# Graph network on one core: the source-order row numbers found in two pieces of columns

## The reference

```python
h = x @ W_in2f
Wij = (ssp(rbf @ Wf1 + bf1) @ Wf2 + bf2) * dist_cut     # rbf: 64 attributes of an edge, dist_cut: its weight
m = segment_sum(h[idx_j] * Wij, idx_i, num_segments=n)  # called with idx_i = src, idx_j = dst
m = ssp(m @ Wo1 + bo1) @ Wo2 + bo2
```

## Time and profile before

| | us |
|---|---|
| median of 3 runs | 6600.42 (6594.85 to 6607.0) |
| the profiled execution | 6596.57 |
| its span | 6594.8 |
| PE / DVE / ACT / POOL busy in the span | 4219.8 / 3130.8 / 1818.7 / 4481.3 |
| POOL's 416 source scatters (L570), busy | 455.7, mean 1.10 |

### The profile page before, as it was taken

How to read it: one execution, slowest core, us unless ns; L and a number is a source line. 1 busy time by engine, 2 the same in 40 slices (tenths; PEclk the granted TensorE clock), 3 DMA queues, 4 the chain that set the end, 5 groups by cost and what they waited for, 6 DMA issues and landing times. The chain is left out here.

```text
span 6594.8 us, 75926 instructions
## 1 busy us (share of the span) xinstructions
PE 4219.8 (64%) x20428; PEld 2957.2 (45%) x20491; DVE 3130.8 (47%) x6389; ACT 1818.7 (28%) x4089; POOL 4481.3 (68%) x4303
## 2 busy tenths in 40 slices
PE   3000788888876666577697555455578867886554
PEld 2000566666544544366595333333344445554333
DVE  9500455555458888866645322232234444442223
ACT  1000566666435555366373000000000000000000
POOL 3777777777668888455421777677677757776775
PEclk6555899999889899799898677766778889987786
DMA  3111222222146666455201555555566644444333
GB/s 86 45 53 53 70 74 75 75 75 74 23 149 211 211 212 213 131 144 148 63 1 64 162 161 163 152 161 163 145 187 199 206 134 148 147 149 103 102 99 94
DMA packets 450732, 812.01 MB, mean 123 GB/s; under 512 B 144428, under 2 KB 300041, under 8 KB 443916
## 3 DMA queue, kind: packets, MB, share of 16 engines
q0 software_dynamic: 209808, 566.12, 30.4%
q1 hardware_dynamic: 240636, 242.29, 11.6%
HBM read 650.48 MB, written 157.63 MB: 123 GB/s over the span
## 5 line engine op out<-in xcount | busy, mean ns | idle before, releaser
L1455 POOL DMA_INDIRECT p_rows<-table,idx_s x1320 | 1285.4, 974 | 574.3 <-issue 377.0
L1500 PE MATMUL p_psA<-p_rows,p_hot 128*128 128x256 bf16 (+1 forms) x4840 | 928.5, 358 | 722.6 <-DMA p_rows<-table,idx_s 534.3
L1500 PEld LDWEIGHTS p_psA<-p_rows,p_hot 128*128 128x128 bf16 (+1 forms) x4840 | 636.1, 137 | 987.9 <-issue 840.2
L570 POOL DMA_INDIRECT rec_s<-p_rec_out,p_row_s x416 | 455.7, 1095 | 223.1 <-issue 126.2
L584 POOL DMA_INDIRECT p_space<-h_table,p_space x440 | 474.2, 1078 | 134.1 <-issue 134.1
L1455 POOL DMA_INDIRECT p_rows<-rel_table,edge_d x440 | 430.7, 979 | 178.9 <-issue 130.1
L1275 POOL DMA_INDIRECT p_rows<-rel_table,edge_d x440 | 437.0, 993 | 161.4 <-issue 133.2
L654 PE MATMUL p_psW<-p_wf,p_upto 128*128 128x256 f32 x1760 | 461.7, 421 | 118.2 <-DVE p_upto L803 117.4
L1739 POOL DMA_INDIRECT p_kg<-kv_table,edge_d x440 | 424.5, 965 | 146.4 <-issue 111.0
L376 POOL DMA_INDIRECT rec_d<-edge_d,norm x416 | 410.9, 988 | 158.3 <-issue 125.9
L1876 DVE TENSOR_REDUCE sums<-p_psM 128x8 f32<-128x1024 f32 x440 | 516.9, 1215 | 2.1 <-PE p_psM L1802 1.8
(11 more groups left out here) (342 smaller groups left out, 8803.2 us busy)
## 6 DMA issues: line engine op xcount, KB each, us to landing
v_sorted<-p_kg SPq DMA_DIRECT2D x110, 512.0 KB, 4.2
p_val<-v_sorted SPq DMA_DIRECT2D x110, 512.0 KB, 3.7
rel_table<-p_o SPq DMA_DIRECT2D x50, 1024.0 KB
p_rows<-table,idx_s POOLq DMA_INDIRECT x1320, 3.1
p_space<-rec_s SPq DMA_DIRECT2D x110, 136.0 KB, 2.1
p_rows<-rel_table,edge_d POOLq DMA_INDIRECT x880, 2.8
p_rec_out<-edge_attr SPq DMA_DIRECT2D x103, 128.0 KB, 2.3
table<-p_o SPq DMA_DIRECT2D x50, 192.0 KB
```

The costliest lines, as they stand in the source:

```text
L570: pool.indirect_dma_start(g.rec_s_rows, bass.IndirectOffsetOnAxis(ap=row_s[:, n * U + u:n * U + u + 1], axis=0), rec_out[q][:, u, :], None ...
L1455: pool.indirect_dma_start(rows[q][:, u, :], None, table, bass.IndirectOffsetOnAxis(ap=idx(n * U + u), axis=0))\
L1500: step = pe.matmul(psA[:, bass.ds(at[u], D)], hot[q][:, u, :], rows[q][:, u, c * D:(c + 1) * D], start=False, stop=(c == terms - 1), skip_ ...
```

## The change

`place_edges` takes a first and a last column (by default all), and works on these alone; the correction of the last column is made only by the piece that has it. The call for the source order becomes two: columns 0 to 31 (FIRST = 8 chunks of 4), then 32 to 415, with a signal of `placed` behind each. The wait for the types and weights (`rest_in`), which stood between the placing and the signal, now stands ahead of the first piece. POOL starts with the first signal, and waits for the second one ahead of the scatters of chunk 8. ACT's wait for the first signal stays as it is. The call for the target order is unchanged.

```diff
+FIRST = 8
-def place_edges(dve, link, g, m, row_out):
+def place_edges(dve, link, g, m, row_out, c0=0, c1=None):
     EC, NB, NT = g.EC, g.NB, g.NT
-    ti = m.tmp_i[:, :]
+    c1 = EC if c1 is None else c1
+    cols = slice(c0, c1)
+    ti, pos, part = m.tmp_i[:, cols], m.pos_f[:, cols], m.part_f[:, cols]
     for b in range(NB):
-        slot = m.part_f if b else m.pos_f
-        of_b = slice(b * EC, (b + 1) * EC)
-        link(dve.scalar_tensor_tensor(out=slot[:, :], in0=m.upto[:, of_b], scalar=m.shift[:, b:b + 1], in1=m.mask[:, of_b],
-                                      op0=ALU.add, op1=ALU.mult))
+        of_b = slice(b * EC + c0, b * EC + c1)
+        link(dve.scalar_tensor_tensor(out=part if b else pos, in0=m.upto[:, of_b], scalar=m.shift[:, b:b + 1],
+                                      in1=m.mask[:, of_b], op0=ALU.add, op1=ALU.mult))
         if b:
-            link(dve.tensor_tensor(m.pos_f[:, :], m.pos_f[:, :], m.part_f[:, :], ALU.add))
+            link(dve.tensor_tensor(pos, pos, part, ALU.add))
...
-    last = row_out[:, EC - 1:EC]
-    link(dve.tensor_tensor(last, last, g.beyond[:, :], ALU.add))
+    if c1 == EC:
+        last = row_out[:, EC - 1:EC]
+        link(dve.tensor_tensor(last, last, g.beyond[:, :], ALU.add))
...
                     pool.wait_ge(brought[q], 16 * (n // few + 1) + 16 * (n == sends - 1))
                     pool.wait_ge(noted, n + 1)
+                    if n == FIRST:
+                        pool.wait_ge(placed, 2)
...
                 find_last(dve, link, g, m, last_tile, ended)
-                place_edges(dve, link, g, m, row_s[:, :])
                 dve.wait_ge(rest_in, 64)
+                place_edges(dve, link, g, m, row_s, 0, FIRST * U)
+                dve.sem_inc(placed, 1)
+                place_edges(dve, link, g, m, row_s, FIRST * U)
                 dve.sem_inc(placed, 1)
```

More of the change, by code:

```diff
@@ L286, in order_blocks @@
     link(dve.tensor_tensor(m.jump[:, 1:NB], m.order[:, 1:NB], m.order[:, 0:NB - 1], ALU.subtract))
-def place_edges(dve, link, g, m, row_out):
+def place_edges(dve, link, g, m, row_out, c0=0, c1=None):
     EC, NB, NT = g.EC, g.NB, g.NT
-    ti = m.tmp_i[:, :]
+    c1 = EC if c1 is None else c1
+    cols = slice(c0, c1)
+    ti, pos, part = m.tmp_i[:, cols], m.pos_f[:, cols], m.part_f[:, cols]
     for b in range(NB):
-        slot = m.part_f if b else m.pos_f
-        of_b = slice(b * EC, (b + 1) * EC)
-        link(dve.scalar_tensor_tensor(out=slot[:, :], in0=m.upto[:, of_b], scalar=m.shift[:, b:b + 1], in1=m.mask[:, of_b],
-                                      op0=ALU.add, op1=ALU.mult))
+        of_b = slice(b * EC + c0, b * EC + c1)
+        link(dve.scalar_tensor_tensor(out=part if b else pos, in0=m.upto[:, of_b], scalar=m.shift[:, b:b + 1],
+                                      in1=m.mask[:, of_b], op0=ALU.add, op1=ALU.mult))
         if b:
-            link(dve.tensor_tensor(m.pos_f[:, :], m.pos_f[:, :], m.part_f[:, :], ALU.add))
-    link(dve.tensor_copy(ti, m.pos_f[:, :]))
+            link(dve.tensor_tensor(pos, pos, part, ALU.add))
+    link(dve.tensor_copy(ti, pos))
     link(dve.tensor_scalar(ti, ti, P - 1, None, ALU.bitwise_and))
-    link(dve.tensor_copy(m.part_f[:, :], ti))
-    link(dve.tensor_copy(ti, m.pos_f[:, :]))
+    link(dve.tensor_copy(part, ti))
+    link(dve.tensor_copy(ti, pos))
     link(dve.tensor_scalar(ti, ti, 7, None, ALU.arith_shift_right))
-    link(dve.scalar_tensor_tensor(out=row_out, in0=m.part_f[:, :], scalar=float(NT), in1=ti, op0=ALU.mult, op1=ALU.add))
-    last = row_out[:, EC - 1:EC]
-    link(dve.tensor_tensor(last, last, g.beyond[:, :], ALU.add))
+    link(dve.scalar_tensor_tensor(out=row_out[:, cols], in0=part, scalar=float(NT), in1=ti, op0=ALU.mult, op1=ALU.add))
+    if c1 == EC:
+        last = row_out[:, EC - 1:EC]
+        link(dve.tensor_tensor(last, last, g.beyond[:, :], ALU.add))
 def find_blocks(dve, link, g, m, plan, found, signal):
```

## The result

Over eight runs of each the changed kernel takes 6623.06 us (6619.68 to 6629.2), the kernel before 6598.17 (6594.39 to 6607.0): 1.0038 times as long, 95% interval 1.0028 to 1.0048. The forecast was 6601.6, from 6590 to 6613, with 0.87 for "within 0.2%". It is slower beyond that. The profiled execution took 6620.07 us, its span 6618.3, which is 23.5 more than before.

The account below looks back on a forecast made before the run. POOL's source scatters were taken as the bound until about 700 us: DVE 10.7 us later, less 9.5 us for 7.4 scatters' lead, gives +1.2 us on the median 6600.42, so 6601.6 us, range 6590 to 6613.

Parts of the forecast that it names:

- The two pieces: DVE's row numbers computed as 32 then 384 columns: 45.5 us against 34.8, so DVE 10.7 us later.
- the upper price: DVE's product on 32 columns at 0.25 us instead of 0.194: DVE 12.2 us later, adding 0.7 us to the sum.
- The first scatter, 16 scatters: POOL starts at 83.9, held by SP's blank records, 16.4 us earlier; 16 scatters at 1.31 us reach 104.9.
- SP: SP's in-order queue still issues chunk 4's load at 122.13, behind fills and stores; it lands 7.3 us later, at 129.4.
- the standstill: POOL stops at 104.9 for chunk 4's attributes and goes on at 130.4: 25.5 us, new.
- The estimate of 2.3 us: Chunk 4's load landing in 2.3 us, not 7.3; the sum would be -1.6 us instead of +1.2.
- The step that failed: POOL's scatters beside DVE's comparisons after the restart: one every 2.27 us, 16.9 from 130.4 to 168.8.
- the slower ones: Cases slower by over 0.2%: SP slowed, chance 0.04, and shifts of DVE's later code, chance 0.02.
- Rival 2: SP's fills slowed by the early scatters, chunk 4's load 21 us later: 6614 us and more; chance 0.04.
- Rival 1: Chunk 4's load comes by 105, so POOL's early start meets no attribute limit: 15.1 us faster, 6585; chance 0.07.
- the sum: Change in the last source scatter's time; with no attribute limit, 10.7 - 25.8 = -15.1 us.

Follow-up runs that it names:

- reordered_third: Changed kernel with SP's fills, bias rows and stores issued between the attribute loads, comparisons unchained, on a quicker chip: 6580.31 us, 0.9977 of the kernel before.
- changed_third: The changed kernel itself, run again on a quicker chip: 6618.74 us, 1.0036 of the kernel before.
- before_pause: Kernel before, in one piece, POOL made to pause ahead of chunk 1 until 14 comparisons are used, on a slower chip: 7297.67 us, 1.0040.
- changed_again: The changed kernel itself, run again on a quicker chip: 6624.09 us, 1.0046 of the kernel before.
- restart_scan2: Kernel before plus 16 blocks of 10 unchained comparisons; POOL waits for its scatters to land, then restarts at varied points; quicker chip: 6730.29 us.
- chained_third: Changed kernel with each comparison waiting for the end of the one before, on a quicker chip: 6574.10 us, 0.9969 of the kernel before.
- eight_buffers: Changed kernel with 8 attribute buffers instead of 4, on a slower chip: 7288.43 us, 1.0021 of the kernel before.
- chained: Changed kernel with each comparison waiting for the end of the one before, on a slower chip: 7271.46 us, 1.0002 of the kernel before.
- late_start: Changed kernel with POOL's first wait for both pieces, so no early scatter, on a slower chip: 7283.87 us, 1.0013 of the kernel before.
- reordered: Changed kernel with SP's fills, bias rows and stores issued between the attribute loads, comparisons unchained, on a slower chip: 7336.36 us, 1.0077 of the kernel before.
- restart_scan: Kernel before plus 16 blocks of 10 unchained comparisons, POOL waiting for PE in each but not for landed scatters, on a slower chip: 7305.17 us.

## Why the prediction was wrong

**The two pieces: right, at the upper price.** The product at 128x32 takes 0.25 us, the end of the prediction's range that it called the upper price, not the 0.194 that it took. DVE is 12.23 us later; it had 10.7, and 12.2 as the bound.

**The first scatter, 16 scatters: right.** 83.74 for 83.9; the 16th at 103.33, so 1.31 us apart on average, as taken. That the average fits is in part luck: the first two scatters took 1.19 and 1.26 us, and from the third on they come every 1.27, although the second piece's products and additions ran beside them.

**SP: right.** The 40 fills take 30.35 us; the load of chunk 4 is issued at 121.41 (122.1), the 17th scatter follows at 129.26 (130.4), 7.9 us behind it, the standstill 24.97 for 25.5. The load landed after 7.6 us, so the price of the earlier trace rows, 7.3, held (SP's timeline):

```profile
121.41 5.96 SPq L492 DMA_DIRECT2D p_rec_out<-edge_attr  x4
```

The estimate of 2.3 us from the Trainium skill (SBUF — State Buffer, The DMA setup-cost knee) would have put the scatter at 124 or 125, and the trace differs.

**The step that failed** is "From 130.4 to the end of the comparisons at 168.8 there are 38.4 / 2.27 = 16.9 scatters". There was one. The rate of 2.27 us was read from a queue of scatters that had been there since the first comparison, and was used for one that comes back 18.1 us into the row. With the measured times that rule gives 41.0 / 2.27 = 18.1 scatters from 129.26 to 170.30, so 34.1 done at the end and a last scatter 12.2 - (34.1 - 25.5) x 1.275 = 1.2 us later, the forecast again. Done were 17: 17.1 fewer, times 1.275 us, 21.8 us. 1.2 + 21.8 = 23.0, and 23.29 were measured. Seen in one step: the kernel before starts its 27th scatter at 159.22, 1.15 us behind the last comparison, the changed one its 18th at 171.44, 1.14 behind it; nine scatters are 11.5 us, and DVE's 12.2 come on top. The 27th in the kernel before:

```profile
159.22 0.97 POOL L570 DMA_INDIRECT rec_s<-p_rec_out,p_row_s  x1 [0.30 <-issue]
```

**The rivals.** None of the slower ones was this. Rival 2 (SP slowed) has the right sign, but SP wasn't slowed in this run. Rival 1's mechanism, "the early start holds", is what SP's other order brings: reordered_third is 15.9 us faster than the kernel before, where the sum gave 15.1. The trace of before had the standstill's place and length in it; what it had no row of was a scatter that starts afresh beside the comparisons, and the prediction gave that no bounds of its own.

**Where the change's gain went.** Of 16.5 us of earlier start 12.2 were paid on DVE; then the standstill (25 us) came, and with it the one lost row. Without the standstill, and with the same unchained row, the kernel is 38 us faster than the changed one (reordered_third against changed_third). With the standstill and a chained row it is 45 us faster; there the cheaper scatters beside the row have a share.

**What stays open.** What in the chip decides that, between 5.4 and 7.4 us of an unchained row without a scatter, the row is no longer entered. The bounds are from one program on a slower chip; before_pause on such a chip fits them (kept out after 7.36 us), and the quicker ones agree as far as they were tried (served up to 4.7 comparisons, or 5.3 us, kept out at 15.9). One instruction was tried, a comparison at 128x1024 with two inputs; other kinds and sizes of unchained rows weren't.

## What to carry to other kernels

A price of an operation beside another engine's row holds for the state in which it was read: ask whether the queue was running when the row began, and whether a pause of it ends in the midst of the row. Where DVE issues a long row of unchained instructions and POOL issues indirect DMAs beside it, look in POOL's timeline for one DMA as long as the rest of the row. If there is one, try a dependence between DVE's instructions: here it cost 0.13 us an instruction and let POOL in. An earlier start of a queue is worth no more than its next supply: find the load that its last buffer waits for, and try moving that too. Try both on each kind of chip: on the slower ones chaining alone ended level with the kernel before, and moving SP's loads made it slower.

## What the hardware showed that was not expected

- **A row is closed to newcomers.** 52 unchained comparisons, 1.135 us apart, let a scatter in at each second one if it was there early, and none at all (some 36 comparisons, 41.87 us) if it came late. Three profiled executions, those of the changed kernel, changed_again and changed_third, show the same 41.87. The Trainium skill (SBUF — State Buffer, SBUF: two separate sides and, below it, A bandwidth-pool intuition that's wrong) describes the pair of ports that DVE and GpSimd share as an exclusive lock, held for one whole instruction, and expects the loser to go on about 0.115 us behind DVE's end. The single scatters of restart_scan2, over some 0.83 us behind a comparison's end where a scatter alone takes 0.97, would fit a lock held until the end of an instruction; no run here shows the lock itself. That a scatter is shut out over one DVE instruction after another for 41.87 us is not in the rule, and the measurement decides.
- **A gap of some 0.03 us opens it.** Unchained, a comparison of 1.225 us starts 1.135 us behind the one before, so 0.09 before that one is over. In chained_third it takes 1.232 and starts 1.27 behind. That was enough: scatters take 0.97 us beside them, as beside an idle DVE, where 1.97 was the price.
- **The slower chips differ in more than speed.** While scatters follow each other at 1.27 us there, others come late: SP's 40 fills take 61.81 us in eight_buffers and 41.58 in chained, where late_start on the same chip, whose first scatter starts when they are all but over, and chained_third on a quicker one both have 30.35. In reordered DVE gets one comparison in 22 us, and goes on so for 27 us behind the last source scatter. A version that is 15.9 us faster on one kind of chip (reordered_third) is 62 us slower on the other (reordered). Why wasn't found.
- **POOL's queue runs ahead of its indirect DMAs**: a wait put behind them didn't show between them (restart_scan, no idle time over 0.8 us), and with a wait for their landing ahead of it POOL stood still for 2.1 to 7.0 us (restart_scan2).
